# Gate and cell order in an LSTM + RNN stack: ScalarE takes both halves' gates before the first cell tanh, VectorE's order follows

## The reference

```python
def _L0_cond_ref(x, h0, Wx, Wh, b):
    c0 = jnp.zeros_like(h0)
    xW = jnp.einsum('ntd,dk->tnk', x, Wx) + b
    def step(carry, xw_t):
        prev_h, prev_c = carry
        a = xw_t + prev_h @ Wh
        i = jax.nn.sigmoid(a[:, :Hdim])
        f = jax.nn.sigmoid(a[:, Hdim:2 * Hdim])
        o = jax.nn.sigmoid(a[:, 2 * Hdim:3 * Hdim])
        g = jnp.tanh(a[:, 3 * Hdim:])
        next_c = f * prev_c + i * g
        next_h = o * jnp.tanh(next_c)
        return ((next_h, next_c), next_h)
def _L1_cond_ref(x, h0, Wx, Wh, b):
    def step(h, xw_t):
        h_next = jnp.tanh(h @ Wh + xw_t)
        return (h_next, h_next)
x = x + _L0_cond_ref(x, cond_1024, L0_cond_Wx, L0_cond_Wh, L0_cond_b)
x = x + _L1_cond_ref(x, cond_1024, L1_cond_Wx, L1_cond_Wh, L1_cond_b)
```

## Time and profile before

| | |
|---|---|
| median of 3 runs | 2323.71 us (2322.61 to 2323.74) |
| the profiled execution | 2324.58 us, of which the span is 2322.7 us |
| granted TensorE clock | 0.99 of full over the span |
| PE busy | 2276.7 us, 98% |
| PEld busy | 1545.2 us, 67% |
| DVE busy | 1894.1 us, 82% |
| ACT busy | 1664.3 us, 72% |
| DMA | mean 23 GB/s |

### The profile page before, as it was taken

One profiled execution on the slowest core, in us unless ns is written; L12 is line 12 of the kernel. 1 busy time (PEld: TensorE's weight loads), 2 busy tenths in 40 slices (PEclk: granted clock), 3 DMA queues, 4 the chain that ended last, 5 costly groups with the idle time before them and its releaser, 6 DMA issues.

```text
span 2322.7 us, 150617 instructions
## 1 busy us (share of the span) xinstructions
PE 2276.7 (98%) x65564; PEld 1545.2 (67%) x65564; DVE 1894.1 (82%) x10283; ACT 1664.3 (72%) x5662; POOL 1.8 (0%) x10
## 2 busy tenths in 40 slices
PE   5999999999999999999999999999999999999997
PEld 2666666666666666666666666666666666666665
DVE  5888888888888888888888888888888888888886
ACT  4777777777777777777777777777777777777775
POOL 0000000000000000000000000000000000000000
PEclk7999999999999999999999999999999999999999
DMA  5000000000000000000000000000000000000000
GB/s 206 8 20 20 23 18 22 13 18 22 23 18 14 22 18 22 22 18 13 18 23 22 18 22 14 18 22 22 18 13 22 18 22 18 22 14 18 22 14 12
DMA packets 16738, 54.03 MB, mean 23 GB/s; under 512 B 2256, under 2 KB 2384, under 8 KB 14800
## 3 DMA queue, kind: packets, MB, share of 16 engines
q1 hardware_dynamic: 16080, 44.41, 5.4%
HBM read 27.62 MB, written 16.78 MB: 19 GB/s over the span
## 4 chain that ended last, share of the span: by engine, by line
PE 95%; DVE 2%; ACT 1%; issue 1%; POOL 0%; DVEq 0%; ACTq 0%; POOLq 0%
PE rec_ps L178 39%; PE in_ps L178 37%; PE rnn_ps L178 19%; ACT wh_part L476 1%; DVE largest_slice L279 0%; DVE turned L355 0%; DVE uv L367 0%; ACT gates_cell L545 0%; DVE h_parts L383 0%; DVE gate_ps L361 0%; DVE h_parts L391 0%; DVE pre_sb L361 0%; DVE gates_cell L372 0%; DVE h_full L384 0%; ACT tanh_c_sb L552 0%
## 5 line engine op out<-in xcount | busy, mean ns | idle before, releaser
L178 PE MATMUL rec_ps<-wh_part,h_parts 128*32 128x256 f16 x32704 | 1011.1, 274 | 6.6 <-DVE h_parts L391 5.5
L178 PE MATMUL in_ps<-wx_sb,x_sb 128*32 128x512 f32 x8192 | 972.1, 594 | 22.7 <-ACT wx_sb L464 22.7
L178 PEld LDWEIGHTS rec_ps<-wh_part,h_parts 128*32 128x32 f16 x32704 | 802.2, 96 | 91.6 <-issue 8.4
L355 DVE STREAM_TRANSPOSE turned<-rec_ps 128x256 f32<-128x256 f32 x1024 | 457.0, 446 | 127.4 <-PE rec_ps L178 127.3
L178 PEld LDWEIGHTS in_ps<-wx_sb,x_sb 128*32 128x32 f32 x8192 | 240.7, 110 | 346.2 <-issue 331.3
L178 PEld LDWEIGHTS rnn_ps<-wx_sb,y 128*32 128x32 f32 x8192 | 235.1, 110 | 316.0 <-issue 314.1
L486 ACT ACTIVATE rec_ps<-in_ps,mask_scaled 128x256 f32<-128x256 f32 x1022 | 406.3, 434 | 1.7 <-PE in_ps L178 1.3
L178 PE MATMUL rnn_ps<-wh_part,h_parts 128*32 128x128 f16 x16352 | 318.1, 220 | 8.6 <-DVE h_parts L419 8.6
L178 PE MATMUL rnn_ps<-wx_sb,y 128*32 128x128 f32 x8192 | 313.1, 273 | 1.8 <-ACT rnn_ps L496 1.6
L545 ACT ACTIVATE gates_cell<-gate_ps,unscale 128x128 f32<-128x128 f32 x511 | 187.9, 368 | 152.6 <-DVE gate_ps L361 120.6
L178 PEld LDWEIGHTS rnn_ps<-wh_part,h_parts 128*32 128x32 f16 x16352 | 281.2, 97 | 11.2 <-ACT rnn_ps L496 5.7
(11 more groups left out here) (52 smaller groups left out, 1403.7 us busy)
## 6 DMA issues: line engine op xcount, KB each, us to landing
x_sb<-xT SPq DMA_DIRECT2D x32, 512.0 KB, 3.8
yT<-y SPq DMA_DIRECT2D x64, 256.0 KB, 2.0
wh_sb<-wh SPq DMA_DIRECT2D x5, 1024.0 KB, 9.3
wx_sb<-wx SPq DMA_DIRECT2D x5, 1024.0 KB, 17.6
b_sb<-b SPq DMA_DIRECT2D x1, 256.0 KB, 2.8
b_sb<-b SPq DMA_DIRECT2D x1, 64.0 KB, 11.8
h_first<-h0T SPq DMA_DIRECT2D x1, 32.0 KB, 19.4
```

Of the source, the lines that this page charges most:

```text
L178: last = nc.tensor.matmul(out[QUAD * q:QUAD * (q + 1)], states, weights(q), start=False, stop=True, tile_position=(0, QUAD * q), skip_grou ...
L355: nc.vector.transpose(turned0[:, half].rearrange("p b n -> p (b n)"), rec0_ps[t % 2][half][:, 0:COLSH]).then_inc(turned0_done[half], 1)
```

## The change

The instructions stay the same; only their order on VectorE and on ScalarE changes. `gates`, `o_half` and `tanh_cell` are the three old instructions of a half, now functions.

ScalarE did gates, output scale and cell tanh of the first half, and then the three of the second. Now it takes the second half's gates between the first half's output scale and its cell tanh, and the second half's output scale behind that tanh.

VectorE now does `state1_high` ahead of `add0` of the second half, `add0(1)` ahead of the first half's gate products, and the second half's gate products and cell ahead of the first half's `state_high`. `state1_low` stands behind the first half's cell, and `add_y1` between the first half's `state_high` and `state_low`.

```diff
@@ -436,18 +436,22 @@
                     turn0(0, t)
                     add0(0, n)
                     turn0(1, t)
+                if rnn_state:
+                    state1_high(s - 1)
+                if lstm:
+                    add0(1, n)
                     gate_products(0, n)
-                    add0(1, n)
                     cell(0, n)
                 if rnn_state:
-                    state1_high(s - 1)
-                    add_y1(s - 1)
                     state1_low(s - 1)
                 if lstm:
+                    gate_products(1, n)
+                    cell(1, n)
                     state_high(0, n)
-                    gate_products(1, n)
+                if rnn_state:
+                    add_y1(s - 1)
+                if lstm:
                     state_low(0, n)
-                    cell(1, n)
                     state_high(1, n)
                     state_low(1, n)
                 if rnn:
@@ -494,6 +498,21 @@
                     act.wait_ge(turned1_done, s)
                 own = (mask_scaled[1] if s else mask)[:, s % PAIR:s % PAIR + 1]
                 nc.scalar.activation(rec1_ps, in1_ps[s // PAIR % 2], ACT.Copy, scale=own).then_inc(seed1_done, 1)
+
+            def gates(half, t):
+                act.wait_ge(pre0_done[half], t + 1)
+                nc.scalar.activation(gates_cell[:, half, 0:GATES].rearrange("p g n -> p (g n)"), pre0[half],
+                                     ACT.Tanh, scale=unscale[0][:, :] if t else 0.5).then_inc(gates_done[half], 1)
+
+            def o_half(half, t):
+                act.wait_ge(gates_done[half], t + 1)
+                nc.scalar.activation(o_scaled[:, half], gates_cell[:, half, 2], ACT.Copy, bias=H_SCALE / 2,
+                                     scale=H_SCALE / 2).then_inc(o_scaled_done[half], 1)
+
+            def tanh_cell(half, t):
+                act.wait_ge(cell_done[half], t + 1)
+                nc.scalar.activation(tanh_c[half], gates_cell[:, half, GATES], ACT.Tanh,
+                                     scale=0.5).then_inc(tanh_c_done[half], 1)
 
             act.wait_ge(b0_in, 16)
             double(g_columns(b0_sb[:, :].rearrange("p (q c) -> p q c", q=1))).then_inc(b0_doubled, 1)
@@ -540,17 +559,12 @@
                     act.wait_ge(seed1_done, s + 1)
                     bias1(s // 2 + 2)
                 if t < STEPS:
-                    for half in range(HALVES):
-                        act.wait_ge(pre0_done[half], t + 1)
-                        nc.scalar.activation(gates_cell[:, half, 0:GATES].rearrange("p g n -> p (g n)"), pre0[half],
-                                             ACT.Tanh, scale=unscale[0][:, :] if t else 0.5).then_inc(gates_done[half], 1)
-
-                        act.wait_ge(gates_done[half], t + 1)
-                        nc.scalar.activation(o_scaled[:, half], gates_cell[:, half, 2], ACT.Copy, bias=H_SCALE / 2,
-                                             scale=H_SCALE / 2).then_inc(o_scaled_done[half], 1)
-                        act.wait_ge(cell_done[half], t + 1)
-                        nc.scalar.activation(tanh_c[half], gates_cell[:, half, GATES], ACT.Tanh,
-                                             scale=0.5).then_inc(tanh_c_done[half], 1)
+                    gates(0, t)
+                    o_half(0, t)
+                    gates(1, t)
+                    tanh_cell(0, t)
+                    o_half(1, t)
+                    tanh_cell(1, t)
 
 
 def kernel(x, cond_1024, L0_cond_Wx, L0_cond_Wh, L0_cond_b, L1_cond_Wx, L1_cond_Wh, L1_cond_b):
```

## The result

| | before | after |
|---|---|---|
| median | 2323.59 us | 2369.25 us (2368.56 to 2369.52) |
| ratio | | 1.0199, 95% interval 1.0187 to 1.0210 |
| span of the profiled execution | 2322.7 us | 2367.6 us |
| median step, `turn0(0)` to `turn0(0)` | 4.400 us | 4.504 us |

The account below looks back on a forecast made before the run. The prediction took the loop through the second half's state (4.40 us a step) as the bound. The first half's loop would become 4.48, adding 0.08 over about 510 steps, +41 us, to 2364 us; range 2348 to 2395.

Parts of the forecast that it names:

- the loop through the second half: PE group 8, group 11, turn0(0), gates and cell, second state_low, next group 8: sets the 4.40 us step before.
- PE's stream: TensorE's own work in a step: 4.35 us of the 4.40, so not the bound before.
- The first half without slack: PE group 0 starts as soon as the first half's state_low allows; delaying that by more than 0.05 us lengthens the step.
- Point 1: VectorE, state1_high between turn0(1) and add0(1): hidden in the wait for the transpose, cost 0, otherwise +0.06 us.
- The rival without overlap: VectorE: state1_high holds up add0(1) by 0.06 to 0.15 us; step 4.54 to 4.63, 2395 us and up; chance 0.07.
- Points 2 to 4: ScalarE and VectorE: gates(1) 0.43 us earlier, first tanh 0.07 to 0.10 later, state1_low at cost 0, cell(1) at 1003.44.
- Point 5: VectorE: state_high(0) behind gate_products(1) and cell(1) makes the first half's state ready 0.13 us later (0.11 to 0.24).
- Point 6: Second half's state_low ends 0.43 us earlier, so PE's 0.05 us hole before group 8 goes.
- the hole ahead of group 8: Gap in PE's weight loads while group 8 waits for the second half's state, about 0.05 us lost each step.
- The sum: Longest of first loop 4.48, PE 4.35, second loop 3.97 us: +0.08 a step, about 510 steps, +41 us.
- The faster rival: Hole goes and the first half's state_low comes at most 0.04 us later; down to 2298 us; chance 0.05.

Follow-up runs that it names:

- b2: Kernel before with half of layer 1's input product left out (8 of 16 matmuls, 0.22 us of PE's stream a step); 2322.11 us.
- a1: Changed kernel with the second half's cell moved behind the first half's second product, and add_y1 behind the first half's state_low; 2300.97 us, ratio 0.9900.
- a3: a1 with the first half's state_high waiting for its tanh alone, the scaled-output-gate wait moved to the earlier state1_low; 2289.18 us, ratio 0.9854.
- b1: Kernel before with one swap on VectorE: the first half's state_low behind the second half's cell; 2412.79 us.
- c1: ScalarE's new order with VectorE's order of the kernel before; 2390.86 us.
- c2: VectorE's new order with ScalarE's order of the kernel before; 2617.51 us.

## Why the prediction was right

- *What bounds before*: the loop through the second half at 4.40, PE's stream at 4.35. b2 shows that PE's stream is not the bound: PE has less to do, the step stays, and group 8's first load still follows the second half's L391 by 0.05. a1 shows that it is the second half's loop: that loop is shorter by 0.24 there, the first half's is no shorter (A is 2.675 against 2.664), and the step falls from 4.400 to 4.363. That PE's stream is 4.35 is shown by a3, which falls with less PE work.
- *The first half without slack*: the decisive reading, from the constant 0.12 between `state_low` and the first load. Shown by b1.
- *Point 1, `state1_high` at no cost*: right, as `state1_high` started at 1023.93, 0.08 before the 256-column transpose's end at 1024.01, and `add0(1)` at 1024.04, 0.03 behind it. The rival without overlap did not come about for this operation. Nor did the headline rule of the Trainium skill (VectorE: DVE Perf Modes, "The DRAIN you can't avoid"), that the next operation starts only once the one ahead has emptied. The same section adds that a next operation that is not held starts earlier, which is what this row shows, so the section as a whole does not speak for the rival as the prediction has it.
- *Points 2 to 4*: `gates(1)` 0.80 behind `turn0(1)`, as forecast. Mis-sized: it lasts 0.40, taken as 0.39 from the earlier trace rows.
- *Point 5, the price*: 0.15 instead of 0.13 (2.816 against 2.664). The prediction's own rows add up to 0.12, since 1003.74 + 0.13 is 1003.87 and not 1003.88. The term has the right place: in the changed kernel the first product starts 0.11 behind `cell(1)` where 0.10 was taken, and the gates give 0.02. `add_y1`'s share was put at 0.02 and is 0.01.
- *Point 6*: the hole ahead of group 8 is gone, the second half's L391 ends 0.45 behind the first's, as forecast.
- *The sum*: 510 x 0.104 = 53 us from the steady step, where 41 were forecast. Measured are 45.7. Two small things outside the steady step go the other way, and the forecast had neither: from the eighth step on, 36 steps of the kernel before are longer than the median by 0.07 to 0.38 us, 7.8 us in sum, and 17 of the changed kernel, 3.2 us in sum, so 4.6 us come back; and its first `turn0` runs 1.2 us earlier (40.35 against 41.59 us). 53 - 4.6 - 1.2 = 47. The last 1 to 2 us are not placed. So the 2364 is as near as it is partly because a step too small by 0.02 met a gain that was not counted: without that gain the time would have been near 2375, and the forecast 11 us short, not 5. The mechanism is shown; that the time came so near is in part luck.
- *The faster rival* failed on the term named there: the first half came 0.15 late, where 0.04 was the limit. Run a1 shows how near it lay: two instructions in another order, and the time is 2301.

## What to carry to other kernels

When a recurrent state is handed over in parts, each part closes its own loop, and bringing the late part forward gains only down to the next loop. Before reordering, measure for each handover the distance from the producer's end to the consumer's start; if it is the same as where the consumer stood idle, that part has no slack, however early it looks beside the other. In an in-order engine, put an instruction that waits for another engine behind the work that is ready before it, and let the wait that has long been met be made by an earlier instruction.

## What the runs showed of the hardware

- A start with two waits costs more than one with one: the first half's product followed its tanh's end by 0.10 us with two waits (a1) and by 0.04 with one (a3), though the second wait had long been met. At TensorE group 0's first matmul, behind two waits, followed its state by 0.15 us (1003.93 to 1004.08), and group 8's, behind one, by 0.06 (1004.94 to 1005.00). On VectorE a1 and a3 differ in nothing else, so that is shown: A fell by 0.07 us and the time by 12 us, 8 of them by the shorter step. On TensorE it is only a comparison of two places; no run changed the number of waits there.
- ScalarE is held for 0.31 us by a 128-column tanh that lasts 0.40 (c1), and for 0.14 us by a 32-column one that lasts 0.20 (1003.05 to 1003.19).
- The gates of the second half last 0.40 us in the changed kernel and 0.39 in the kernel before, with the same operands. In the changed kernel, in a1 and in c1 another ScalarE instruction directly follows without waiting for them. In b1 and c2, where the next one waits for their end, they last 0.39. That fits, but no run was made for it.
- Some steps are longer than the rest, by 0.07 to 0.38 us, and most of them come again every 64 steps: 36, 100, 164, 228 in the kernel before and also in the changed one, others in only one of the two. In the kernel before, from the eighth step on, the first instruction that is late is in 32 of the 36 one of four VectorE instructions, eight times each: the first product (L383) of either half, and the second half's L367 and L391. In the other four it is ScalarE's L467, which runs in every other step, and these four lie 128 steps apart. In one such step of the kernel before, the second half's product starts at 465.97, 0.46 behind the end of its tanh (465.51), where 0.10 is usual. The cause is open; it was not tried.
